# ScalarE's exp of tile k ahead of its f16 copy of tile k-1, in a cross-attention and feed-forward kernel on one core

## What is computed

```python
q = (query @ Wq + bq)...   # from x;  k, v from the context, 16 heads of 32
scores = q k^T / sqrt(32);  allowed = j < i          # strictly causal
attn = softmax(where(allowed, scores, -1e30)); attn of row 0 = 0
x = layer_norm(query + (attn @ v) @ Wo + bo)
out = layer_norm(x + relu(x @ W1 + b1) @ W2 + b2)
```

## Time and profile before

| | |
|---|---|
| median of 3 runs | 2654.29 us (2650.04 to 2656.82) |
| the profiled execution's own time | 2651.14 us |
| its span, first to last instruction | 2649.3 us |
| busy in the whole span | PE 94%, DVE 80%, ACT 62%, POOL 60% |
| busy in the attention part, 96 to 1198 us | PE 1010.38 us, DVE 1007.07 us, ACT 983.58 us, POOL 810.97 us of 1102 us |
| granted TensorE clock | 0.989 |

### The profile page before, as it was taken

How to read it: one execution, slowest core, us unless ns; L and a number is a source line. 1 busy time by engine, 2 the same in 40 slices (tenths; PEclk the granted TensorE clock), 3 DMA queues, 4 the chain that set the end, 5 groups by cost and what they waited for, 6 DMA issues and landing times.

```text
span 2649.3 us, 62863 instructions
## 1 busy us (share of the span) xinstructions
PE 2498.2 (94%) x22664; PEld 1873.3 (71%) x22664; DVE 2116.9 (80%) x4886; ACT 1629.8 (62%) x2881; POOL 1585.5 (60%) x1721
## 2 busy tenths in 40 slices
PE   4899999999999999879999999999999999999998
PEld 1455555555555555557888888888888888888887
DVE  7999999999999999878767777767767676767675
ACT  2788889899899999886344444343444343444433
POOL 2677777777777777666455555555555555554543
PEclk9999999999999999989999999999999999999999
DMA  5344444443344443345232313222222222222220
GB/s 169 110 117 117 119 114 110 115 109 103 92 103 105 106 106 97 89 140 159 53 69 50 71 46 67 50 69 53 66 56 61 61 57 64 57 65 57 65 57 25
DMA packets 444456, 225.04 MB, mean 85 GB/s; under 512 B 302368, under 2 KB 388192, under 8 KB 444144
## 3 DMA queue, kind: packets, MB, share of 16 engines
q1 hardware_dynamic: 442544, 219.71, 32.5%
q10 hardware_dynamic: 1600, 1.31, 0.2%
HBM read 112.36 MB, written 57.69 MB: 64 GB/s over the span
## 4 chain that ended last, share of the span: by engine, by line
PE 63%; DVE 8%; SPq 8%; POOL 8%; issue 7%; DMA 4%; ACT 1%; ACTq 0%; DVEq 0%; POOLq 0%
PE h_ps L1646 23%; PE acc L1662 20%; POOL prob_lo L495 7%; PE front L1632 6%; PE lin_ps L934 5%; SPq L421 4%; PE max_ps L907 2%; PE st_ps L955 2%; DVE max_ps L886 2%; PE lin_ps L930 1%; PE o_ps L973 1%; SPq L458 1%; SPq L1065 1%; DMA heads<-stage 1%; PE st_ps L986 1%
## 5 line engine op out<-in xcount | busy, mean ns | idle before, releaser
L495 POOL TENSOR_TENSOR prob_lo<-probs,prob_hi 128x512 f16<-128x512 f32 (+1 forms) x768 | 797.8, 1047 | 335.2 <-ACT prob_hi L582 318.5
L1646 PE MATMUL h_ps<-x_halves,W 128*128 128x256 f16 x6144 | 756.2, 273 | 1.8 <-ACT hf L1431 1.7
L1662 PE MATMUL acc<-W,hs 128*128 128x256 f16 x5376 | 669.6, 273 | 0.3 <-DVE hs L1599 0.3
L1646 PEld LDWEIGHTS h_ps<-x_halves,W 128*128 128x128 f16 x6144 | 596.5, 98 | 87.5 <-issue 14.8
L1431 ACT ACTIVATE hf<-h_ps,b1s,scale_evac 128x256 f32<-128x256 f32 x512 | 284.9, 563 | 559.7 <-PE h_ps L1646 557.2
L1662 PEld LDWEIGHTS acc<-W,hs 128*128 128x128 f16 x5376 | 526.0, 98 | 61.4 <-DVE hs L1599 0.6
L1356 POOL TENSOR_TENSOR hf<-hf 128x256 f32<-128x256 f32 x256 | 243.4, 951 | 483.1 <-ACT hf L1431 482.7
L588 ACT ACTIVATE probs<-st_ps,exp_scale 128x512 f32<-128x512 f32 (+1 forms) x768 | 469.3, 611 | 98.2 <-PE st_ps L986 91.6
L886 DVE CUSTOM_DVE_ANT_0 max_ps<-max_ps,mask_q 128x256 f32<-128x256 f32 (+2 forms) x768 | 418.2, 560 | 47.1 <-PE max_ps L907 43.4
L582 ACT ACTIVATE prob_hi<-probs 128x512 f16<-128x512 f32 (+1 forms) x768 | 427.9, 557 | 23.0 <-issue 7.3
L1599 DVE TENSOR_TENSOR hs<-hf,hs 128x896 f16<-128x896 f32 x256 | 282.0, 1121 | 147.8 <-ACT hs L1420 147.7
(11 more groups left out here) (152 smaller groups left out, 3526.1 us busy)
## 6 DMA issues: line engine op xcount, KB each, us to landing
heads<-stage SPq DMA_DIRECT2D x748, 64.0 KB, 2.1
raw_c<-in_cT SPq DMA_DIRECT2D x64, 256.0 KB, 3.4
raw_x<-in_xT SPq DMA_DIRECT2D x64, 256.0 KB, 4.4
o_in<-ctx_rows SPq DMA_DIRECT2D x256, 64.0 KB, 2.5
x_in<-in_x SPq DMA_DIRECT2D x32, 512.0 KB, 4.0
x_rows<-x SPq DMA_DIRECT2D x64, 256.0 KB, 2.1
o_in<-x_rows SPq DMA_DIRECT2D x256, 64.0 KB, 2.4
out<-y SPq DMA_DIRECT2D x32, 512.0 KB, 3.0
```

The lines of the kernel that those rows point to most:

```text
L495: pool.tensor_tensor(prob_lo[:, k % 4, 0:w], probs[:, k % PROBS, 0:w], prob_hi[:, k % 4, 0:w], ALU.subtract).then_inc(pl_done, 1)
L1646: last = pe.matmul(h_ps[:, f % 2, 0:T], W1[:, aw, j, f * P:(f + 1) * P], x1_halves[:, item.parity, aa, j, :], start=(j == 0 and m == 0), s ...
L1662: last = pe.matmul(acc_products[:, n, :], hs[:, p % HS, aa, n, :], W2[:, p, aw, n, :], start=(p == 0 and m == 0 and n % 2 == 0), stop=(p = ...
```

## The change

In ScalarE's slot the two blocks are swapped. Both keep their slots (`ST_AT` for the exp, `ST_AT + 1` for the copy), their waits, their tiles and their rings; so in one slot ScalarE does first the exp of tile k and then the copy of tile k-1, where it did the copy of tile k-1 first and the exp of tile k after it. The evictions and splits of the slot stay ahead of both.

```diff
-                for item, k in due(window, s, SLOTS, B, ST_AT + 1, SLOTS):
-                    w = ST_WIDTH[k % 3]
-                    wait_for(act, exp_done, SLOTS, item, k + 1)
-                    wait_for(act, pv_done, SLOTS, item, k + 1 - 4)
-                    act.activation(prob_hi[:, k % 4, 0:w], probs[:, k % PROBS, 0:w], ACT.Copy).then_inc(ph_done, 1)
                 for item, k in due(window, s, SLOTS, B, ST_AT, SLOTS):
                     w = ST_WIDTH[k % 3]
                     wait_for(act, st_done, SLOTS, item, k + 1)
                     wait_for(act, pl_done, SLOTS, item, k + 1 - PROBS)
                     at = item.n % 3
                     act.activation(probs[:, k % PROBS, 0:w], st_ps[:, k % 2, 0:w], ACT.Exp, bias=PROB_BIAS,
                                    scale=exp_scale[:, at:at + 1]).then_inc(exp_done, 1)
+                for item, k in due(window, s, SLOTS, B, ST_AT + 1, SLOTS):
+                    w = ST_WIDTH[k % 3]
+                    wait_for(act, exp_done, SLOTS, item, k + 1)
+                    wait_for(act, pv_done, SLOTS, item, k + 1 - 4)
+                    act.activation(prob_hi[:, k % 4, 0:w], probs[:, k % PROBS, 0:w], ACT.Copy).then_inc(ph_done, 1)
                 yield
```

## The result

The changed kernel takes 2723.99 us (median), the kernel before 2654.3 us: ratio 1.0268, 95% interval 1.0255 to 1.0282, **70 us slower**. The forecast was slower, by 48 us, range 2664 to 2738. The forecast named a real part of the loss and sized its chain to 0.01 us. But only some 31 of the 70 us go when that chain is given time; the rest is owed to two things that it had counted at nothing, and that the number still falls into the range is partly luck.

What follows compares the result with a forecast made beforehand. VectorE bounds tiles 3 to 23 of an item, TensorE those from 24 on. Late values 2.8 + 0.6 - 0.3 = 3.1 us per item, less about 0.1, times 16 give 48 us: 2654.3 to 2702 us, range 2664 to 2738.

Steps and rivals of the forecast that it cites:

- What bounds the kernel: Attention item: VectorE sets the pace from tile 3 to 23, TensorE from tile 24 on; TensorE never waits for `prob_lo`.
- GpSimd as a follower of ScalarE's copy: GpSimd isn't full: it idles between operations until ScalarE's copy arrives, 256.4 us in all; its busy time should stay.
- The chain of 2.63 us: From masks of tile k+1 through exp, copy and `prob_lo` to values of tile k, a head's first tile: 2.63 us.
- First tiles only: Only each head's first tile makes values late; nothing counted for second and third tiles, whose way is shorter.
- 2.8 + 0.6 us per item: Late values at nine heads' first tiles cost 2.8 us; ScalarE falling behind at tiles 43, 46 and 34 adds 0.6.
- 3.1 against 3.5 us per item: Forecast loss per item was 3.1 us: 2.8 + 0.6, less 0.3 taken from TensorE's wait for heads.
- Evictions at nothing: Evictions and splits up to 0.52 us later on ScalarE: counted at nothing, 24 us at worst at the wait for heads.
- VectorE's stretch hides its seven heads: TensorE's 3.7 us wait for maxima there absorbs seven heads' late values; not hidden, 1.9 us per item.
- the rival without any absorption: VectorE's stretch hides nothing: all sixteen heads pay, 4.9 us per item, 1.9 of it there; chance 0.18, evictions included.
- ScalarE's saved gaps at no gain: 479 copies lose a 0.14 us gap, 67 us of ScalarE's time; no gain, since ScalarE waits for TensorE's scores.
- the second rival: ScalarE's time is the price about tiles 42 to 3: saved gaps give 15 us, 2639 us; chance 0.06.
- The rival of 2733 us: All sixteen heads pay, in VectorE's stretch too: 79 us, or 2757 us with 24 us of late evictions; chance 0.18.

## Why the prediction was right or wrong, by its own steps

- **What bounds the kernel.** Two stretches an item, TensorE's and VectorE's: held. GpSimd as a follower of ScalarE's copy: held, it waits for the copy 250.3 us. That its busy time would stay did not hold: it fell from 1585.5 to 1556.0 us, and no run says why.
- **The chain of 2.63 us.** Right: 2.63 in the rows above, 2.62 in the mean at most first tiles. Six steps, each from a row of the kernel before, added to the right number; in the rows after, each is within 0.01 us of what it was taken for.
- **First tiles only.** Mostly right. Of the twenty-odd tiles an item whose values now start within 0.2 us of their `prob_lo`, fifteen or sixteen are first tiles. Giving these their old order takes back 50 us, though it changes the place of some evictions too.
- **2.8 + 0.6 us per item from it.** The 2.8 came: the nine distances outside VectorE's stretch grew from 20.9 to 23.7 us. The 0.6 did not: ScalarE was to start the exps of tiles 43, 46 and 34 0.26, 0.24 and 0.10 us late, and in items 1 to 14 all three start 0.04 us behind their masks.
- **3.1 against 3.5 us per item is partly luck.** Of the 3.5 in items 8 to 13, 2.4 lie outside tiles 3 to 22, where all 3.1 were expected, and 1.1 inside, where none was. Read by cause instead, from the runs with a slot more: 2.2 us for the chain (31 us of the 70 in the whole), 2.5 for the place of evictions and splits, less 1.2 for ScalarE's saved gaps. Terms left out on both sides happened to cancel.
- **Evictions at nothing.** This step failed ("I count nothing in the middle and 3 x 0.5 x 16 = 24 us at worst"). I had argued that VectorE has 1.6 us of waits to take the delay from, and named 24 us as the worst, at the moves of heads. It cost about 25 us where the chain has time (both runs with a slot more), and on another path: VectorE's lo part stands ahead of its maxima, and TensorE waits for these; the wait for heads fell to 0.2 us. VectorE, busy 92% of 100 to 1150 us, had idle time in some slots, which did not help in those where the evictions fall.
- **VectorE's stretch hides its seven heads.** Partly. In items 8 to 13 tiles 3 to 22 lose 1.1 us, in items 1 to 6 0.3 us; the rival without any absorption said 1.9.
- **The first seven items.** Missed, 1.7 us per item. I had followed the moved copy past ScalarE's own neighbours but not `prob_lo` past GpSimd's additions, which stand behind it in the same stream, and through them SyncE's queue. The steps of that path are read from rows; that the low clock comes with the longer stall is borne out by the run with the stores moved, where that slot has neither.
- **ScalarE's saved gaps at no gain.** Right for this kernel: its busy time fell by 28 us, the idle time before the copy from 23.0 to 0.0 us, and the exp's wait for scores rose by more than both. They aren't worthless: with a slot more for the values and the evictions ahead, items 8 to 13 take 1.2 to 1.3 us less than in the old order with the same slots. This is the second rival's mechanism, hidden under two costs.
- **The rival of 2733 us** (all heads pay) has the nearest number and a part of the cause: of its 1.9 us in VectorE's stretch 1.1 came in items 8 to 13, and the 24 us for late evictions that it adds on top are near the 25 measured, though not at the wait for heads. The first items are in neither.
- **Left open.** How the last item's 9 us divide; which part of the 34 us is the splits' and which the copy right behind its exp; and the three shares, 31, 25 and 15 us, are read in one order of undoing and would differ in another, since chain and evictions are tied.

## What to carry to other kernels

Swapping two operations in a slot so that dependent neighbours become independent saves the engine a gap, and lengthens the way to the consumer by the wait for the next tile. Add up that way step by step and compare it with what the consumer's engine gives it now, tile shape by tile shape. Then do the same for everything else that stands in the stream: an operation that is pushed behind the moved one, on its own engine and on each engine that follows it, needs its own slack, in its own slot. A mean of idle time, and a worst case put at one place only, say nothing about that.

## What the runs showed that I had not expected

- A copy that follows its own exp starts 0.03 us after the exp's end; one that follows another tile's starts 0.10 us before it. The Trainium skill ("ScalarE: Activation LUTs", section "What ACT_TABLE_LOAD costs") has the overlap of about 93 ns; the gap of the dependent pair is this case's.
- Ahead of tile 24 in items 1 to 6, an idle time of TensorE of 0.9 to 1.4 us (kernel before) was followed by full clock six times of six, one of 2.5 to 2.8 us (kernel after) by the lower level six times of six, at a price of 1.0 us. The length alone does not decide it: in item 0 of the kernel after full clock followed 2.5 us, with first tiles copied ahead the lower level followed 1.8 us in item 6, and with the change and evictions ahead full clock followed 2.6 us in item 4.
- One slot more between scores and values cost the kernel before 0.51%, though hardly any wait for `prob_lo` was there to be saved. The sums of the output move to other slots of VectorE with it, which is the likely cause and was not tested by itself. Distance wasn't free here.
